# Third attention: the output projection turned round, and its two closing stages made one

## What is computed

```python
def fq_act(t, s):
    q = jnp.clip(jnp.round(t / s) + ZP, 0.0, 255.0)      # ZP = 128
    return (q - ZP) * s
...
o = jnp.einsum('bhnm,bhmd->bhnd', attn, v)
o = o.transpose(0, 2, 1, 3).reshape(B, N, C)
o = fq_act(o, s_a2)
o = o @ fq_weight(w_proj, sw_proj).T + b_proj
return fq_act(o, s_a3)
```

## Time and profile before

| what | us |
|---|---|
| median of 3 runs | 2308.22 (2302.86 to 2309.53) |
| the profiled execution | 2315.61 |
| its span in the profile | 2313.9 |
| busy in the span: PE, DVE, ACT, POOL | 1693.8, 1288.6, 1053.5, 343.5 |
| the two closing stages, first to last DVE instruction | 1584.49 to 1620.64 |

### The profile page before, as it was taken

The page is one execution under the profiler, slowest core; times in us unless marked ns, Lnnn a source line. Parts: engine busy times, 40 slices in busy tenths (PEclk is TensorE's granted clock), DMA queues, the critical chain, the costliest instruction groups (busy, mean ns, idle before and its releaser), DMA issues. The chain is left out here.

```text
span 2313.9 us, 36221 instructions
## 1 busy us (share of the span) xinstructions
PE 1693.8 (73%) x12222; PEld 1368.8 (59%) x12238; DVE 1288.6 (56%) x2687; ACT 1053.5 (46%) x2190; POOL 343.5 (15%) x415
## 2 busy tenths in 40 slices
PE   3588879957842499966499676653893798479995
PEld 2265666846631255555499554443783698479995
DVE  6588865252157789968523559997217210643223
ACT  4466754233325578865222247883322354322221
POOL 0000000005730000001242100000000342034431
PEclk9798978979975699987699787775996699689998
DMA  4200010034540000001576200000003453457775
GB/s 85 74 10 18 19 31 13 2 98 132 167 155 1 4 7 6 4 1 26 167 226 203 78 4 8 7 3 1 13 1 120 151 184 114 134 163 222 226 212 191
DMA packets 137247, 189.85 MB, mean 82 GB/s; under 512 B 51661, under 2 KB 111213, under 8 KB 137069
## 3 DMA queue, kind: packets, MB, share of 16 engines
q1 hardware_dynamic: 116289, 146.91, 20.8%
q0 software_dynamic: 15360, 36.72, 5.4%
q10 hardware_dynamic: 5420, 3.91, 0.6%
HBM read 150.21 MB, written 33.68 MB: 79 GB/s over the span
## 5 line engine op out<-in xcount | busy, mean ns | idle before, releaser
L1014 DVE TENSOR_TENSOR 36_l3f_mlp_hidden<-36_l3f_mlp_gate,36_l3f_mlp_first 128x512 f32<-128x512 f32 x51 | 35.0, 687 | 173.7 <-ACT 36_l3f_mlp_gate L992 106.6
L1270 PE MATMUL 2_performer_p_u<-perf_proj,2_performer_yT 128*87 128x512 f32 (+1 forms) x204 | 96.5, 618 | 10.6 <-DVE 2_performer_arg L1431 9.4
L907 PE MATMUL 36_l3f_mlp_first<-36_l3f_mlp_xT,36_l3f_mlp_w 128*128 128x128 f32 x816 | 101.1, 278 | 0.0
L907 PEld LDWEIGHTS 36_l3f_mlp_first<-36_l3f_mlp_xT,36_l3f_mlp_w 128*128 128x128 f32 x816 | 96.9, 195 | 0.0
L1030 DVE TENSOR_SCALAR 9_l0f_mlp_y<-9_l0f_mlp_second,l0f_routing_weight 128x192 f32<-128x192 f32 x51 | 21.2, 417 | 112.2 <-DMA l0f_results<-9_l0f_mlp_y,l0f_routing_put 84.5
L992 ACT ACTIVATE 36_l3f_mlp_gate<-36_l3f_mlp_first 128x512 f32<-128x512 f32 x51 | 30.5, 597 | 115.9 <-PE 36_l3f_mlp_first L912 115.9
L1028 DVE TENSOR_TENSOR 32_l3a_mlp_y<-32_l3a_mlp_second,l3a_experts_b_rows 128x192 f32<-128x192 f32 x29 | 10.4, 358 | 130.6 <-issue 96.1
L921 PE MATMUL 36_l3f_mlp_second<-l3f_experts_w,36_l3f_mlp_hidden 128*128 x408 | 79.9, 339 | 0.0
L2643 ACT ACTIVATE l1a_p<-14_pla_f,l1a_recip 128x87 int16<-128x87 f32 x272 | 71.7, 354 | 9.2 <-DVE l1a_recip L2718 9.2
L1014 DVE TENSOR_TENSOR 22_l1f_mlp_hidden<-22_l1f_mlp_gate,22_l1f_mlp_first 128x512 f32<-128x512 f32 x29 | 19.9, 687 | 100.3 <-ACT 22_l1f_mlp_gate L992 100.3
L988 ACT ACTIVATE 32_l3a_mlp_hidden<-32_l3a_mlp_first,l3a_experts_b_cols 128x128 f32<-128x128 f32 x174 | 48.1, 375 | 60.1 <-PE 32_l3a_mlp_first L912 59.9
(11 more groups left out here) (930 smaller groups left out, 4957.0 us busy)
## 6 DMA issues: line engine op xcount, KB each, us to landing
36_l3f_mlp_w<-in_L_ffn_w_dram SPq DMA_DIRECT2D x51, 768.0 KB
22_l1f_mlp_w<-in_L_ffn_w_dram SPq DMA_DIRECT2D x29, 768.0 KB, 4.6
32_l3a_mlp_w<-in_L_attn_W_dram SPq DMA_DIRECT2D x29, 576.0 KB, 3.9
9_l0f_mlp_w<-in_L_ffn_down_w_dram SPq DMA_DIRECT2D x51, 192.0 KB
l3a_experts_w<-in_L_attn_W_dram SPq DMA_DIRECT2D x8, 576.0 KB, 8.3
l1a_blocks<-l1a_qkb SPq DMA_DIRECT2D x192, 5.4 KB, 1.8
l1f_experts_w<-in_L_ffn_w_dram SPq DMA_DIRECT2D x8, 384.0 KB, 6.2
l2a_blocks<-l2a_qkb SPq DMA_DIRECT2D x192, 5.4 KB, 1.8
```

What stands on the lines that cost most here:

```text
L907: nc.tensor.matmul(to(t + a * PAIRS), of[:, t + a * PAIRS, :], at[:, 0, :], start=(t == 0), stop=True, skip_group_check=True)
L1014: v.tensor_tensor(hidden[j % 2][:], gate[j % 2][:], first[j % 2][1][:, 0, 0:HT, :], ALU.mult).then_inc(hidden_done, 1)
L1270: ins = t.matmul(p_u[:, k, 0:(EIGHT - h) * M], yT[b % 2][:, k, :], proj[:, h:EIGHT, :].rearrange("p h m -> p (h m)"), start=True, stop=True)
```

## The change

Stages 3 and 4 of the list become one, `l2a_close_stage`. `store` no longer adds MAGIC but writes int32, which rounds; `CX` becomes int32 and DVE cuts a group into its bf16 slot in one instruction. As soon as the groups that hold them are in `CT`, pieces of 256 tokens (11 of them, the last one shorter) are projected with `WP` as weights and the tokens streaming, so that 96 output channels x 256 tokens lie in PSUM, in two halves. Scale and bias are now one number for each partition: ACT applies both and rounds to int32 in one instruction for each half (`scale_up`); the factors sw_proj x s_a2 / s_a3 and b_proj / s_a3 are worked out with the constants, from two small columns (`out_cols`) that are loaded in place of the broadcast bias row. DVE cuts the piece to bf16 (`limit`), PE turns it back with four transposes into bf16 in PSUM (`turn_back`), and DVE multiplies by s_a3 and adds to `H` out of PSUM (`add`), followed by the two tiles' `bn_stats`. The additions of a piece stand behind the `limit` of the next piece on DVE, and turning back a piece stands behind the projection of the next one on PE. The weights' rows on 128 partitions stay; the multiplication of them by s_a2 goes. The loads are 14 instead of 13.

```diff
--- before.py
+++ after.py
@@ -1564,6 +1564,8 @@
         a[name] = in_pairs(a[name])
     for name in ("L1_attn_bq", "L1_attn_bk"):
         a[name + "_cols"] = a[name].reshape(HALVES, KP).T
+    a["L2_attn_sw_proj_cols"] = a["L2_attn_sw_proj"].reshape(HALVES, KP).T
+    a["L2_attn_b_proj"] = a["L2_attn_b_proj"].reshape(HALVES, KP).T
     a["L2_attn_b_qkv_cols"] = a["L2_attn_b_qkv"][0:2 * D].reshape(2 * HALVES, KP).T
     a["L3_ffn_norm_w"] = in_columns(a["L3_ffn_norm_w"])
     a["L3_ffn_w13"] = in_pairs(a["L3_ffn_w13"].transpose(0, 2, 1))
@@ -3459,7 +3461,7 @@
 
             def store(j):
                 dve.wait_ge(weighed, j + 1)
-                v.tensor_scalar(out[:, 2 * j:2 * j + 2, :], p_out[:, :, 0:D], to_int, MAGIC, ALU.mult, ALU.add).then_inc(stored, 1)
+                v.tensor_scalar(out[:, 2 * j:2 * j + 2, :], p_out[:, :, 0:D], to_int, None, ALU.mult).then_inc(stored, 1)
 
             v.memset(ps[:], 0.0).then_inc(cleared, 1)
             v.tensor_scalar(minus[:], kit.identb[:], -1.0, None, ALU.mult).then_inc(cleared, 1)
@@ -3484,7 +3486,7 @@
 def l2a_constants(link, v, early):
 
 
-    wq, wp, sw, rows, cols, v_row, s4, con, WP, rsw, rsp, low = early
+    wq, wp, sw, rows, cols, v_row, s4, con, WP, rsw, rsp, low, out_cols = early
     W3 = 3 * D
 
     def ts(out, in_, a, b, o0, o1=None):
@@ -3509,7 +3511,7 @@
             link(v.tensor_tensor(w[:], w[:], across(scale, 1, HALVES), ALU.mult))
     inv = low[:, 0:4]
     link(v.reciprocal(inv, s4[:]))
-    s1, s_attn, s2, s3 = (s4[:, j:j + 1] for j in range(4))
+    s1, s_attn, _, s3 = (s4[:, j:j + 1] for j in range(4))
 
     ts(con[:, 0:1], s1, s1, float(DH) ** -0.5, ALU.mult, ALU.mult)
     ts(con[:, 0:1], con[:, 0:1], inv[:, 1:2], None, ALU.mult)
@@ -3537,7 +3539,8 @@
     ts(con[:, 13:14], con[:, 13:14], t1, None, ALU.subtract)
     ts(t0, con[:, 5:6], con[:, 5:6], 0.25, ALU.mult, ALU.mult)
     ts(con[:, 14:15], con[:, 6:7], t0, None, ALU.subtract)
-    ts(rows[:, 0, :], rows[:, 0, :], s2, None, ALU.mult)
+    ts(out_cols[:, 0, :], out_cols[:, 0, :], s4[0:KP, 2:3], inv[0:KP, 3:4], ALU.mult, ALU.mult)
+    ts(out_cols[:, 1, :], out_cols[:, 1, :], inv[0:KP, 3:4], None, ALU.mult)
     ts(cols[:], cols[:], inv[0:KP, 0:1], None, ALU.mult)
     ts(v_row[:], v_row[:], inv[0:KP, 0:1], None, ALU.mult)
 
@@ -3710,77 +3713,160 @@
             dve.wait_ge(v_cut, NB // EIGHTH)
 
 
+def l2a_close_stage(kit, H, stats, CX, WP, out_cols, scale):
+
+
+
+
+
+    nc = kit.nc
+    GROUP, EVEN_ROWS = 4, 88
+    GROUPS = NB // GROUP
+    SPAN = 2 * TP
+    PIECES = TN // 2
+    with kit.stage("l2a_close") as ctx:
+        CT = kit.sb(ctx, "cT", [KP, HALVES, TOKENS], BF16)
+        slot = [kit.sb(ctx, f"slot{u}", [NT, GROUP, D], BF16) for u in range(2)]
+        whole = [kit.sb(ctx, f"whole{u}", [KP, HALVES, SPAN], I32) for u in range(2)]
+        limited = [kit.sb(ctx, f"limited{u}", [KP, HALVES, SPAN], BF16) for u in range(2)]
+        turned = [kit.ps(ctx, f"turned{u}", [KP, HALVES, 1024], BF16) for u in range(2)]
+        p_o = [kit.ps(ctx, f"p_o{u}", [KP, HALVES, SPAN]) for u in range(2)]
+        back = [kit.ps(ctx, f"back{u}", [TP, 2, 512], BF16) for u in range(2)]
+        staged, turned_done, evacuated, projected, rounded, limited_ready, back_done, added, stats_done = (
+            kit.sem(ctx, n) for n in ("staged", "turned_done", "evacuated", "projected", "rounded", "limited_ready",
+                                      "back_done", "added", "stats_done"))
+        block = ctx.enter_context(nc.Block(no_gpsimd_drain=True))
+        wide = lambda q: min(SPAN, TOKENS - q * SPAN)
+        upto = [min((g + 1) * GROUP * NT // SPAN, PIECES) if g < GROUPS - 1 else PIECES for g in range(GROUPS)]
+        pieces_of = lambda g: range(upto[g - 1] if g else 0, upto[g])
+        rows_of = lambda i: TP if i < TN - 1 else LAST
+
+        @block.tensor
+        def _(pe):
+
+            def turn(g):
+                pe.wait_ge(staged, g + 1)
+                if g >= 2:
+                    pe.wait_ge(evacuated, g - 1)
+                for n in range(GROUP):
+                    for k in range(HALVES):
+                        ins = nc.tensor.transpose(turned[g % 2][:, k, n * EVEN_ROWS:n * EVEN_ROWS + NT],
+                                                  slot[g % 2][:, n, k * KP:(k + 1) * KP], kit.identb[0:NT, 0:NT])
+                ins.then_inc(turned_done, 1)
+
+            def project(q):
+                if q >= 2:
+                    pe.wait_ge(rounded, q - 1)
+                at = slice(q * SPAN, q * SPAN + wide(q))
+                for h in range(HALVES):
+                    for k in range(HALVES):
+                        ins = nc.tensor.matmul(p_o[q % 2][:, h, 0:wide(q)], WP[:, k, h * KP:(h + 1) * KP], CT[:, k, at],
+                                               start=(k == 0), stop=(k == 1))
+                ins.then_inc(projected, 1)
+
+            def turn_back(q):
+                pe.wait_ge(limited_ready, q + 1)
+                if q >= 2:
+                    pe.wait_ge(added, 2 * (q - 1))
+                for u in range(2):
+                    n = rows_of(2 * q + u)
+                    for h in range(HALVES):
+                        ins = nc.tensor.transpose(back[q % 2][0:n, u, h * KP:(h + 1) * KP],
+                                                  limited[q % 2][:, h, u * TP:u * TP + n], kit.identb[0:KP, 0:KP])
+                ins.then_inc(back_done, 1)
+
+            turn(0)
+            for g in range(GROUPS):
+                if g + 1 < GROUPS:
+                    turn(g + 1)
+                pe.wait_ge(evacuated, g + 1)
+                for q in pieces_of(g):
+                    project(q)
+                    if q >= 1:
+                        turn_back(q - 1)
+            turn_back(PIECES - 1)
+
+        @block.scalar
+        def _(act):
+
+            def evacuate(g):
+                act.wait_ge(turned_done, g + 1)
+                w = GROUP * NT
+                out = CT[:, :, g * w:(g + 1) * w].rearrange("p k (n t) -> p k n t", n=GROUP)
+                of = turned[g % 2][:, :, 0:GROUP * EVEN_ROWS].rearrange("p k (n t) -> p k n t", n=GROUP)
+                nc.scalar.activation(out, of[:, :, :, 0:NT], ACT.Copy).then_inc(evacuated, 1)
+
+            def scale_up(q):
+                act.wait_ge(projected, q + 1)
+                if q >= 2:
+                    act.wait_ge(limited_ready, q - 1)
+                for h in range(HALVES):
+                    ins = nc.scalar.activation(whole[q % 2][:, h, 0:wide(q)], p_o[q % 2][:, h, 0:wide(q)], ACT.Identity,
+                                               bias=out_cols[:, 1, h:h + 1], scale=out_cols[:, 0, h:h + 1])
+                ins.then_inc(rounded, 1)
+
+            evacuate(0)
+            for g in range(GROUPS):
+                if g + 1 < GROUPS:
+                    evacuate(g + 1)
+                for q in pieces_of(g):
+                    scale_up(q)
+
+        @block.vector
+        def _(dve):
+            v = nc.vector
+
+            def stage_group(g):
+                if g >= 2:
+                    dve.wait_ge(turned_done, g - 1)
+                v.tensor_scalar(slot[g % 2][:], CX[:, g * GROUP:(g + 1) * GROUP, :], -128.0, 127.0, ALU.max,
+                                ALU.min).then_inc(staged, 1)
+
+            def limit(q):
+                dve.wait_ge(rounded, q + 1)
+                if q >= 2:
+                    dve.wait_ge(back_done, q - 1)
+                v.tensor_scalar(limited[q % 2][:, :, 0:wide(q)], whole[q % 2][:, :, 0:wide(q)], -128.0, 127.0, ALU.max,
+                                ALU.min).then_inc(limited_ready, 1)
+
+            def add(q):
+                dve.wait_ge(back_done, q + 1)
+                for i in range(2 * q, 2 * q + 2):
+                    n = rows_of(i)
+                    v.scalar_tensor_tensor(H[0:n, i, :], back[q % 2][0:n, i % 2, 0:D], scale[0:n, :], H[0:n, i, :], ALU.mult,
+                                           ALU.add).then_inc(added, 1)
+                for i in range(2 * q, 2 * q + 2):
+                    dve.wait_ge(added, i + 1)
+                    v.bn_stats(stats[:, i, :], H[:, i, :]).then_inc(stats_done, 1)
+
+            stage_group(0)
+            stage_group(1)
+            for g in range(GROUPS):
+                if g + 2 < GROUPS:
+                    stage_group(g + 2)
+                for q in pieces_of(g):
+                    limit(q)
+                    if q >= 1:
+                        add(q - 1)
+            add(PIECES - 1)
+            dve.wait_ge(stats_done, TN)
+
+
 def l2_attn(kit, H, stats, early, loads):
     nc, dram = kit.nc, kit.dram
     W3 = 3 * D
     with ExitStack() as outer:
         def sb(n, s, dt=F32, ctx=outer):
             return ctx.enter_context(nc.sbuf_tensor("l2a_" + n, s, dt))
-        wq, wp, sw, rows, cols, v_row, s4, con, WP = early[0:9]
+        con, WP, out_cols = early[7], early[8], early[12]
         QKB = sb("qkb", [KP, 2, HALVES, TOKENS], BF16)
```

(13 more changed lines are left out.)

48 lines of the change are left out of this document (removed).

## The result

The changed kernel takes 2296.9 us (median of 22 runs) where the kernel before, run beside it, takes 2305.9 (22 runs). The ratio is 0.9951, 95% interval 0.9937 to 0.9965, so 11.3 us less, with an interval of 8.1 to 14.5. The ratio is an estimate of its own, without the few executions in which the chip was in a slower state; the two medians by themselves lie 9.0 us apart (0.9961). The forecast was 7.8 us less and 2300.4 us, the range 2295.5 to 2305.0. The sign was right and the gain was forecast too small.

What follows compares the result with a forecast made beforehand. VectorE's chain was taken to bound the two closing stages (36.15 us). Work 22.9 plus waits 2.9 and 1.9, taken as 27.8, gains 8.35; constants cost 0.6; 2308.2 - 7.8 = 2300.4 us, range 2295.5 to 2305.

Steps and rivals of the forecast that it cites:

- the loop's 1.9: Closing stage: VectorE waits 0.8 us before cut 1, 0.7 before cut 5 and 0.4 before cut 8, 1.9 us together.
- a round of 3.3: Closing stage: turning back, projecting, scaling and cutting, with four steps between engines, take 3.3 us for two pieces.
- The steps between the engines: Closing stage: each hand-over from one engine to another costs 0.05 us, read from the front stage.
- VectorE's work, 22.9 us forecast: Closing stage: stagings 4.2, cuts 4.6, sums 8.1 and statistics 6.0 us make 22.9; upper bound without overlap 25.4.
- terms (a) to (c): VectorE's closing-stage work: (a) 8 stagings 4.2 us, (b) 11 cuts 4.6 us, (c) 22 sums out of PSUM 8.1 us.
- the constants: Front stage of the ffn before: one more load 0.46 us, changed multiplications 0.15; +0.6 us, bounds 0.1 and 0.9.
- The hand-overs that bind: Closing stage: steps of 0.1 us and sums of 0.435 let the two-piece loop set the pace; 30.3 us, 2303 whole; chance 0.20.
- The clock that rises: Closing stage: TensorE's clock rises, its times halve and the loop drops out; 26.3 us, 2299 whole; chance 0.18.
- The chain of double buffers: Closing stage: buffers don't overlap, each piece runs as one chain of 4.65 us; 54 us, 2327 whole; chance 0.02.
- no gain: Closing stage: VectorE's work at its bound and waits doubled, 25.4 + 9.6 = 35.0 us, 2308 whole; chance 0.05.

## Why the prediction was right and wrong

**Right: where, and what stays.** VectorE's chain sets the stretch, before and after. One stage of 26.05 us took the place of 36.15, with the waits at 4.99 us (4.8 forecast: 2.9 at the start, measured 0.49 + 2.42, and 1.9 in the loop, measured 2.08). That the loop's 1.9 came so near is in part luck: it was the difference of a round of 3.3 and two pieces of 1.70, and both were too large, by 0.4 each (2.92, and 2 x 1.50). The steps between the engines, 0.05 each, held. ScalarE's 557 ns, the projection's 1.07 for four and TensorE's 20.16 us (19.4) came as worked out; turning back took 0.50 to 0.53 in place of 0.63. The sums out of bf16 in PSUM take what they take out of f32 (405 ns, and 0.40 in the earlier trace rows). The barrier stayed (2.05), and the int32 store takes 607 ns as before.

**Wrong: VectorE's work, 22.9 us forecast and 21.06 measured.** The step that failed is the pace at which VectorE's instructions follow each other, terms (a) to (c) of its work: each overlaps the one before by 0.08 us where it waits for nothing, and the prediction granted the sums 0.035, the cuts nothing, and the stagings what a pair that waits for itself leaves. For the sums the reading was "Eight 350 ns operations take 2.52 us, so one overlaps the next by 0.035". Those eight additions were not VectorE's own pace. Each needed two matmuls of 0.158, 0.316 together, and from start to start the additions take (2.52 - 0.35) / 7 = 0.31: TensorE set it. Later runs of the same line, in the trace of the kernel before:

```profile
1599.95 2.26 DVE L3771 TENSOR_TENSOR l2a_out<-27_l2a_project_p_o,l2a_rows 128x192 f32<-128x192 f32 x8
...
1600.36 2.74 PE L3750 MATMUL 27_l2a_project_p_o<-l2a_wp,l2a_cT 96*128 96x192 bf16 x16 [1.23 <-DVE l2a_out L3771]
...
1608.86 1.66 DVE L3771 TENSOR_TENSOR l2a_out<-27_l2a_project_p_o,l2a_rows 128x192 f32<-128x192 f32 x6
```

Of the next eight, four had their matmuls done (24 for the first twelve tiles); those of the other four run beside them, and by the trace's single records only the last addition still waits for one, 0.313 behind its neighbour where the six steps before it are 0.265. The last six are 0.262 apart, (1.66 - 0.35) / 5. Against 345 to 350 ns that is an overlap of 0.08 (the 0.077 in the expectation for the changed order came from the whole 2.26, the fed one included). The statistics of the earlier trace rows said the same ((2.17 - 0.34) / 7 = 0.26 apart, 0.08), and so does every pair of neighbours after where the second waits for nothing: two sums in 0.73 (405 ns, 0.325 apart), two statistics in 0.60 to 0.61 (0.26), a cut of 417 ns followed 0.34 later, two stagings in 1.02 (0.47 apart).

The stagings were read from a pair, 1.07 from one group to the next, and halved. The pair's second instruction stands between the two rows shown there:

```profile
1585.08 0.56 DVE L2376 TENSOR_SCALAR 26_l2a_cq_slot<-l2a_cx 87x768 bf16<-87x768 f32 x1
```

It waits for the one before, 0.59 from start to start (1584.49, 1585.08); the next group's first waits for nothing and follows after 0.48 (1585.56). A staging that waits for no neighbour costs the 0.48, not 0.53.

Counted again with these paces: 8 x 0.47 + 11 x 0.34 + 22 x 0.325 + 22 x 0.26 = 20.4, and some 0.5 for the instructions that come after a wait and overlap with nothing. The term was too large by 0.95 at the sums, 0.9 at the cuts (0.42 each, a whole duration), 0.45 at the stagings and 0.3 at the statistics. The run with the order changed bears the size out: 22 overlaps lost, and a stretch 1.68 us longer. Of the signs by which the prediction would have known itself wrong (sums clearly over 0.4, waits for turning back, constants over 1 us) none came; it had none for VectorE's pace. The Trainium skill's "Vector Engine (DVE) Microarchitecture Reference", "Measured stream behaviour on trn2", puts it as 1.04 ns an element and about 75 ns for each instruction once they overlap, which is 275 ns for 192 elements, an estimate: the additions' 265 and the statistics' 260 nearly agree, the sums with a scalar operand have 325 and lie above it, and the stagings, 768 elements in 470 ns where the same estimate gives 875, lie far below it.

**Too large: the constants.** 0.6 was forecast. 0.2 is shown, and the load's 0.46 is lost in the 0.8 by which the start of the constants varies.

**The anchor.** The forecast stood on 2308.22, the middle of three runs; 22 runs have 2305.9, 2.3 lower, which the prediction had named as possible and put into the range on the low side. Put together, the closing stretch gives 1.75 more than forecast and the constants at most 0.4, so 9.5 to 9.9 in place of 7.8, within the 8.1 to 14.5 measured. The 1.4 to 1.8 us up to the middle of that interval, the 11.3, have no place in the traces that can be called shown, and they need not be real: the two medians are 9.0 apart. One candidate stands open: stage 31 of the kernel before, far behind this change, has 21.4 us in two traces of four with the old projection (18.3 in the others), and 18.3 in all eight traces with the new one; nothing in these runs says why. So of the 5.8 us between the forecast 2300.4 and the 2294.6 by the ratio, the anchor has 2.3, the closing stretch 1.75, the constants at most 0.4, and 1.4 to 1.8 are open.

**The rivals.** The hand-overs that bind (30.3 us): false, a step is 0.05 and a piece without waiting takes 1.50. The clock that rises (26.3 us): the length came out near it by chance, but the granted clock is 0.50 in the whole stage, with TensorE busy in 20.16 of 26.10 us, 77%. The chain of double buffers (54 us) and no gain (35.0) are false.

## What to carry to other kernels

Before an engine's pace is taken from a run of equal instructions, ask whether another engine fed it: take the time from start to start and hold it against the producer's pace. If the two agree, it is the producer's number, and another run of the same line, later, has the engine's own. Ask too whether the second of two neighbours needs the first's result, and, where two engines each wait for the other, add up the loop through their buffers before one of them is called the slow one (1.77 us for two groups above). On a stage bound by many short instructions, the order that lets independent neighbours stand side by side costs nothing and was worth 1.7 us of 27.7 here, and idle time at the seam of two stages can take the first steps of the second (2.15 us of 26.05 here).

## What the hardware showed beyond that

In these traces VectorE's instructions overlap their neighbours by 0.08 us (0.075 to 0.087) whatever they are (343 to 546 ns, from SBUF or from PSUM, int32, bf16 or f32) if the second waits for nothing; a second one that waits for the first starts 0.035 us after its end.

TensorE's clock stayed at 0.50 through the closing stage, in which TensorE was busy 20.16 of 26.10 us, in pieces with short pauses. In the tail with the turning moved there, 17 transposes and 24 more ran without a pause from 1568.16 to 1572.12; the granted clock is 0.59 over 1570.1 to 1572.6 and 1.00 in the 1.3 us behind it. The 24 products that follow took 1.18 us, where the kernel with the stagings alone moved, with a pause of 2.46 us ahead of them, took 1.93 at 0.50, and from the first of the 17 transposes to the attention's last store it was 0.75 us less (5.72 and 6.47). The rows of that kernel:

```profile
1569.32 1.93 PE L2819 MATMUL 25_log_int_p_out<-l2a_vb,25_log_int_wT 87*87 87x16 bf16 x24 [2.46 <-ACT 25_log_int_wT L3382]
1569.30:1571.30 2.00, 1.93 (x24) 1.84 (x24) 0.01 (x1) 0.00 (x0) 0.00 (x0) 0.50 0.00 0
```

The clock rose behind these turnings in the one trace there is of this kernel. That they caused it is likely and not shown, since no run varied it alone.
